# Causal attention weighs the values with unsplit exponentials in full 32-bit products on 32 rows

## The reference, cut to what matters

```python
qkv = hidden_states @ Wqkv            # 4 batches, 512 tokens, 512 features
q = qkv[..., :512].reshape(4, 512, 32, 16)          # 32 heads of 16
k = qkv[..., 512:528]                 # one key head and
v = qkv[..., 528:]                    # one value head for all
scores = jnp.einsum('bqhd,bkd->bhqk', q, k) * 16 ** -0.5
scores = jnp.where(causal, scores + alibi, -1e30)
probs = jax.nn.softmax(scores, axis=-1)
attn = jnp.einsum('bhqk,bkd->bqhd', probs, v).reshape(4, 512, 512)
x = x + attn @ Wo
```

## Time and profile before

| | |
|---|---|
| Median of 3 runs | 3246.93 us (3245.48 to 3249.31) |
| Profiled execution, span | 3252.0 us |
| Causal attention's units, 4 batches | from 118 to 728 us of the span |
| Feed-forward, first | about 760 to 1227 us |
| Window attention | about 1227 to 2785 us |
| TensorE busy in the whole span | 2840.8 us, 87% |
| Granted TensorE clock, mean | 0.936 of full speed |

### The profile page before, as it was taken

One profiled execution on the slowest core, in us unless ns is written; L12 is line 12 of the kernel. 1 busy time (PEld: TensorE's weight loads), 2 busy tenths in 40 slices (PEclk: granted clock), 3 DMA queues, 4 the chain that ended last, 5 costly groups with the idle time before them and its releaser, 6 DMA issues. The chain is left out here.

```text
span 3252.0 us, 44782 instructions
## 1 busy us (share of the span) xinstructions
PE 2840.8 (87%) x14364; PEld 2215.5 (68%) x14404; DVE 2248.5 (69%) x4342; ACT 1390.3 (43%) x2947; POOL 1253.5 (39%) x938
## 2 busy tenths in 40 slices
PE   3798888984988896999999997799999999699888
PEld 2564545543766774788888885688888887577666
DVE  3656565644877775878787774778777787577776
ACT  2477666772322224444444443444444444232222
POOL 2266454561422222444444441444444442242221
PEclk7699988986999998999999998999999999799999
DMA  4231414224000001111010010011111100300001
GB/s 151 62 95 33 130 32 124 40 53 136 1 1 1 0 0 54 33 33 32 26 32 10 29 33 27 7 33 33 32 32 32 32 19 1 96 1 1 0 0 52
DMA packets 148429, 125.24 MB, mean 39 GB/s; under 512 B 18644, under 2 KB 117972, under 8 KB 148276
## 3 DMA queue, kind: packets, MB, share of 16 engines
q1 hardware_dynamic: 148308, 123.75, 13.7%
HBM read 96.71 MB, written 27.26 MB: 38 GB/s over the span
## 5 line engine op out<-in xcount | busy, mean ns | idle before, releaser
L1273 POOL TENSOR_TENSOR a_probs_low<-a_probs,a_probs_high 128x512 fp32r<-128x512 f32 x240 | 309.3, 1297 | 329.0 <-ACT a_probs_high L1193 328.0
L1944 POOL TENSOR_TENSOR rope_straight<-rope_straight,rope_crossed 128x512 f32<-128x512 f32 x160 | 206.9, 1293 | 477.8 <-DVE rope_crossed L1755 477.8
L634 POOL TENSOR_TENSOR f_hidden_low<-f_hidden,f_hidden_high 128x512 fp32r<-128x512 f32 x112 | 144.7, 1292 | 552.5 <-ACT f_hidden_high L579 552.5
L1049 DVE TENSOR_REDUCE a_max<-a_max_scores 128x1 f32<-128x384 f32 (+3 forms) x352 | 215.7, 637 | 153.4 <-PE a_max_scores L924 149.7
L1849 ACT ACTIVATE probs<-probs,exp_bias 128x256 f32<-128x256 f32 (+1 forms) x512 | 240.8, 471 | 168.4 <-DVE exp_bias L1737 168.1
L1596 PE MATMUL proj<-y_high,wq_high 128*128 128x512 f32 x512 | 213.3, 417 | 26.3 <-DVE y_low L1725 17.1
L1191 ACT ACTIVATE a_probs<-a_scores 128x512 f32<-128x512 f32 x320 | 192.7, 602 | 97.7 <-PE a_scores L937 48.4
L1596 PE MATMUL w_sum<-o_high,wo_high 128*128 128x512 f32 x512 | 204.2, 399 | 7.6 <-DVE xt L1779 4.7
L1910 ACT CAST probs_turned_high<-probs_turned 128x896 fp32r<-128x896 f32 x128 | 116.3, 908 | 211.9 <-PE probs_turned L1638 211.9
L1856 ACT CAST q_high<-rope_straight 128x512 fp32r<-128x512 f32 x128 | 79.5, 621 | 292.4 <-POOL rope_straight L1944 292.4
L1596 PE MATMUL proj<-y_low,wq_high 128*128 128x512 f32 x512 | 204.0, 399 | 0.0
(11 more groups left out here) (256 smaller groups left out, 8674.1 us busy)
## 6 DMA issues: line engine op xcount, KB each, us to landing
a_queries<-a_q_stacked SPq DMA_DIRECT2D x16, 1024.0 KB, 7.1
wq_raw<-in_L_attn_b_wq SPq DMA_DIRECT2D x32, 512.0 KB, 3.7
wo_raw<-in_L_attn_b_wo SPq DMA_DIRECT2D x16, 1024.0 KB, 6.2
a_q_stacked<-a_q_part_high SPq DMA_DIRECT2D x32, 256.0 KB
a_out_parts<-a_out SPq DMA_DIRECT2D x128, 64.0 KB
f_w_raw<-in_L_ffn_w SPq DMA_DIRECT2D x28, 256.0 KB, 5.3
f_w_raw<-in_L_ffn_w2t SPq DMA_DIRECT2D x14, 512.0 KB, 7.9
a_z<-a_out_parts SPq DMA_DIRECT2D x12, 512.0 KB
```

The costliest lines, as they stand in the source:

```text
L1049: e.tensor_reduce(to, scores, AX.X, ALU.max).then_inc(s["max_read"], 1)
L1273: e.tensor_tensor(pl[:, g % 4], pf[:, g % 4], f32(ph[:, g % 4]), ALU.subtract)\
L1944: e.tensor_tensor(ra[:, slot], ra[:, slot], rb[:, slot], ALU.add).then_inc(roped, 1)
```

## The change

The exponentials are no longer split. ScalarE makes one exponential for each unit, of type float32, and nothing is subtracted from it. The values are no longer split either: the tile has 32 columns, 0 to 15 the values and 16 to 31 ones. TensorE multiplies the two float32 tiles in one product per unit, where two products of float32r tiles stood. The result has one part and its sum in row 16; one store, one load and one addition less follow from that.

```diff
-VROWS = 80
+VROWS = 32
...
-        o_dram = nc.dram_tensor("a_out_parts", [NB, 2, AH * AD, S], F32).ap()
+        o_dram = nc.dram_tensor("a_out_raw", [NB, AH * AD, S], F32).ap()
...
-        vs, vn = sb("a_values", [P, ST, VROWS], F32R), sb("a_values_next", [P, ST, VROWS], F32R)
+        vs, vn = sb("a_values", [P, ST, VROWS]), sb("a_values_next", [P, ST, VROWS])
...
         pf = sb("a_probs", [P, 4, S])
-        ph, pl = (sb(f"a_probs_{x}", [P, 4, S], F32R) for x in ("high", "low"))
...
-                e.wait_ge(*split_by(b, g))
-                for x in (ph, pl):
-                    mm = e.matmul(obank[hg % 2][0:VROWS, :], vs[:, kt, :], x[:, g % 4, :], start=kt == 0 and x is ph,
-                                  stop=kt == qt and x is pl)
-                mm.then_inc(s["pv_done"], 1)
+                e.wait_ge(s["exp_done"], b.it * UB + g + 1)
+                e.matmul(obank[hg % 2][0:VROWS, :], vs[:, kt, :], pf[:, g % 4, :], start=kt == 0, stop=kt == qt)\
+                    .then_inc(s["pv_done"], 1)
...
-            def low_probs(b, g):
-                e.wait_ge(s["exp_done"], b.it * UB + g + 1)
-                e.tensor_tensor(pl[:, g % 4], pf[:, g % 4], f32(ph[:, g % 4]), ALU.subtract)\
-                    .then_inc(s["low_by_vector"], 1)
...
-                chain(e.tensor_tensor(at[:, 0], at[:, 0], at[:, 1], ALU.add))
-                e.tensor_tensor(at[:, 0], at[:, 0], at[:, 2], ALU.mult).then_inc(s["at_ready"], 1)
+                e.tensor_tensor(at[:, 0], at[:, 0], at[:, 1], ALU.mult).then_inc(s["at_ready"], 1)
...
-                if g >= 4 or not b.first:
-                    before = (b, g - 4) if g >= 4 else (Batch(b.it - 1), g - 4 + UB)
-                    e.wait_ge(*split_by(*before))
-                e.activation(pf[:, g % 4], sbank[g % 2][:, :], ACT.Exp)
                 wait(e, s["pv_done"], b.it * UB + g - 3)
-                e.activation(ph[:, g % 4], sbank[g % 2][:, :], ACT.Exp).then_inc(s["exp_done"], 1)
+                e.activation(pf[:, g % 4], sbank[g % 2][:, :], ACT.Exp).then_inc(s["exp_done"], 1)
...
-                        if g % 4 != 1:
-                            low_probs(b, g)
...
-                for c in range(2):
-                    to = o_dram[bass.ds(b.it, 1), c, tile * P:(tile + 1) * P, qt * P:(qt + 1) * P]\
-                        .rearrange("b (h d) q -> d (b h) q", d=AD)
-                    e.dma_start(to, ot[32 * c:32 * c + AD, tile % 2].rearrange("p a h q -> p (a h) q"))\
-                        .then_inc(o_stored[tile % 2], 16)
+                to = o_dram[bass.ds(b.it, 1), tile * P:(tile + 1) * P, qt * P:(qt + 1) * P]\
+                    .rearrange("b (h d) q -> d (b h) q", d=AD)
+                e.dma_start(to, ot[0:AD, tile % 2].rearrange("p a h q -> p (a h) q")).then_inc(o_stored[tile % 2], 16)
...
-                e.dma_start(at[:, 0:2, :], o_dram[bass.ds(b, 1), :, m * P:(m + 1) * P, :].rearrange("b c p t -> p (b c) t"))\
+                e.dma_start(at[:, 0, :], o_dram[bass.ds(b, 1), m * P:(m + 1) * P, :].rearrange("b p t -> (b p) t"))\
```

More of the change, by code:

```diff
@@ L705, in causal_attention @@
         with ExitStack() as late:
-            last_at = sb_in(nc, late)("a_last_out", [P, DT, 3, S])
+            last_at = sb_in(nc, late)("a_last_out", [P, DT, 2, S])
         qa = sb("a_queries", [P, PAIRS, S], F32R)
@@ L716, in causal_attention @@
         vt = sb("a_v_by_dim", [AD, S])
-        at = zf[:, 0:3]
+        at = zf[:, 0:2]
         sums = sb("a_sums_tile", [P, AH * S // P])
@@ L726, in causal_attention @@
         misc = [ps(f"a_misc{i}", [P, S]) for i in range(2)]
-        names = ("max_full", "max_read", "scores_full", "exp_done", "low_by_vector", "low_by_pool", "pv_done", "o_copied",
-                 "misc_used", "m_high", "m_low", "kv_high", "kv_low", "vt_copied", "v_high", "v_low", "q_high", "q_low",
+        names = ("max_full", "max_read", "scores_full", "exp_done", "pv_done", "o_copied",
+                 "misc_used", "m_high", "m_low", "kv_high", "kv_low", "vt_copied", "v_high", "q_high", "q_low",
                  "k_landed", "keys_kept", "x_summed", "sq_ready", "sq_added", "centred", "seed", "z_ready", "zh_ready", "zl_ready",
@@ L821, in group_end @@
             return qt * HG + hg if kt == qt else None
[L823 to L827, removed]
         def wait(e, sem, value):
@@ L991, in read_small @@
                     e.wait_ge(s["v_high"], b.ahead() + 1)
-                    e.tensor_tensor(vn[:, :, 32:32 + AD], bank[:, 0:ST * AD].rearrange("p (t d) -> p t d", t=ST),
-                                    f32(vn[:, :, 0:AD]), ALU.subtract).then_inc(s["v_low"], 1)
-                    e.wait_ge(s["v_low"], b.ahead() + 1)
                     e.sem_inc(free, 1)
@@ L1080, in keep_keys @@
                 e.tensor_copy(ka[1][:, :], kan[1][:, :]).then_inc(s["keys_kept"], 1)
-                e.wait_ge(s["v_low"], b.it + 1)
+                e.wait_ge(s["v_high"], b.it + 1)
                 e.tensor_copy(vs[:, :, :], vn[:, :, :]).then_inc(s["keys_kept"], 1)
             def body(b):
-                chain = Chain(e, s["dve_step"], 3 if b.first else b.it * 7 - 1)
+                chain = Chain(e, s["dve_step"], b.it * 3 + 3)
                 keep_keys(b)
@@ L1103, in body @@
                             if OUT <= g < OUT + OUT_STEP * DT and (g - OUT) % OUT_STEP == 0:
-                                out_tile((b.it - 1) * DT + (g - OUT) // OUT_STEP, chain)
+                                out_tile((b.it - 1) * DT + (g - OUT) // OUT_STEP)
                             if OUT < g <= OUT + OUT_STEP * DT and (g - OUT) % OUT_STEP == 1:
@@ L1109, in body @@
                         read_small(b, *x, chain)
-                    if kind == "scores" and x[0] % 4 == 2:
-                        low_probs(b, x[0] - 1)
             first = Batch(None)
@@ L1119, in _ @@
                 if x[0] == "Vt":
-                    e.wait_ge(s["cleared"], 4)
+                    e.wait_ge(s["cleared"], 3)
                 for j in range(GROUPS[x[1] % ST]) if x[0] == "mT" else ():
@@ L1136, in _ @@
             batches(e, body)
-            chain = Chain(e, s["dve_step"], 7 * NB - 4)
+            chain = Chain(e, s["dve_step"], 3 * NB)
             invert_sums(NB - 1)
             for m in range(DT):
-                out_tile((NB - 1) * DT + m, chain, last_at[:, m], last_landed[m])
+                out_tile((NB - 1) * DT + m, last_at[:, m], last_landed[m])
             for m in range(DT):
@@ L1199, in copy_out @@
                 if hg % 2 == 0:
-                    wait(e, o_stored[hg // 2 % 2], 48 * (b.it * 2 * ST + group_end(g) // 4))
+                    wait(e, o_stored[hg // 2 % 2], 32 * (b.it * 2 * ST + group_end(g) // 4))
                 e.copy(ot[:, hg // 2 % 2, hg % 2], obank[hg % 2][0:VROWS, :].rearrange("p (h q) -> p h q", h=4))\
@@ L1296, in _ @@
                 sum_squares(first, n)
-            e.memset(f32(vn[:, :, 0:64]), 0.0).then_inc(s["cleared"], 1)
-            e.memset(f32(vn[:, :, 64:VROWS]), 1.0).then_inc(s["cleared"], 1)
+            e.memset(vn[:, :, AD:VROWS], 1.0).then_inc(s["cleared"], 1)
             for d in range(DT):
```

12 lines of the change are left out of this document (4 added, 8 removed).

## The result

The changed kernel takes 3322.85 us (median of 4 runs, 3322.25 to 3323.48); the kernel before took 3248.12 us beside it (3245.48 to 3252.44). The ratio is 1.0226, with an interval of 1.0212 to 1.0239: 74.7 us slower, where 34 us were forecast. The profiled execution has a span of 3320.4 us.

A forecast was written before the change was run, and what follows sets the result against it. TensorE was taken as busiest but also waiting in causal attention. Terms +112 - 53 - 7 - 5 - 6 gave +41 us, a second account +27; the middle, +34, gave 3281 us, range 3257 to 3317 (chance 0.69), outer range 3243 to 3345.

The forecast's parts named there:

- The product: TensorE's weighing in causal attention: one float32 product costs 0.35 us a unit more than the pair, +112 us over 320 units.
- The change of shape: Switching TensorE between 32-column and 128-column stationary tiles: taken as 0, with 20 us kept for the range.
- The first rival, the drain: Every product drains TensorE, 0.25 to 0.35 us each, 80 to 112 us in all; 3361 to 3393 us; chance 0.10.
- The waits and slack: TensorE's waits for other engines in the attention stage give back 53 us, slack in short pieces 7 us.
- The sign I gave: In the changed profile, TensorE's listed waits in the stage should fall from 82 to about 35 us.
- The clock: Half speed on some 105 us of the stage costs about 35 us; 5 us taken back, bounds 0 and 35.
- three causes for half speed: Half speed comes at batch starts and behind long waits; three of its causes were said to stay.
- The tail: After the last batch: half the a_out bytes, no addition and no last units' subtraction save 6 us.
- The short slack: Where ScalarE pressed as hard as TensorE, some 65 units gain 0.1 us each, 7 us.
- The second rival: Faster: exchange between engines sets the stage, all waits and half speed go; -29 us, 3218 us; chance 0.08.
- three signs of being wrong: L943's two records under 0.7 us; next instruction over 0.1 us late as a rule; half speed far from 105 us.

The follow-up runs named there:

- e4: Kernel before (two float32r products, 80 columns) with one exponential, no subtractions, low parts left out: 3155.9 us, ratio 0.9697.
- e6: Changed kernel with the values' stationary tile padded from 32 to 80 columns, still one float32 product a unit: 3243.4 us, ratio 0.9962 to the kernel before.
- e3: Changed kernel with exponentials and values in float32r, each unit weighed twice with the same 32-column tiles: 3158.7 us, ratio 0.9700 to the kernel before.
- e5: Changed kernel, 32 columns, with two units' weighings back to back after every odd unit: 3295.0 us, ratio 1.0118 to the kernel before.

## Why the prediction went as it did

The direction held, the likeliest size did not: 34 us forecast, 75 measured, inside the range. Point by point:

- **The product, +112 us.** Right: 108 to 115 us by e4 and e6, 0.453 us from record to record for 0.43.
- **The change of shape, 0.** This step failed. The prediction took L903's hand-over in 0.03 us as what a 32-column tile costs, and gave "the new product has 512 in each of several passes" as the reason why even less would show. L903 is a transpose. The reading of its row was right: it runs without a gap in the changed kernel too, at all 14 places. (In the kernel before only 2 of 14 show the 0.03 us; at 10 others L937 starts just 0.05 us after an exponential has ended, so it waits for ScalarE there, though no gap is listed.) But the row is of another kind of instruction. The product of float32 on 32 columns pays 0.09 us ahead (0.160 for 0.066 in e6) and 0.20 us behind (0.523 + 0.34 us for 0.028 + 0.64), 0.30 us in all. Unit by unit, where both traces are at full clock and without a wait, the changed kernel takes 0.30 us more than e6 too (300 units). The stage got 79 us longer for it, not 96, in part because TensorE idles 8.5 us less. The row nearest to it was L898: a float32 product with a stationary tile of 16 rows by 128 columns, so narrow the other way, with the same shape of price: it starts 0.10 us late, and the product behind it takes 0.38 us for 0.23.
- **The first rival, the drain,** had the mechanism, at 0.25 to 0.35 us a product and 80 to 112 us. Its time, 3361 to 3393 us, is too long mainly because the relief was undersized: the drain itself measured 79. I gave it 0.10 since "the neighbour with 32 columns and 128 rows shows none of it". I had weighed the shape and never the type or the kind of the product.
- **The waits and slack, -60 us.** About right. TensorE idles 66 us less in e6 than before (16.0 us, against 609.8 - 527.3 = 82.5 us of the stage; some 40 missing records of before may make up to 10 us of that). The relief by itself, in e4, brought 43; the rest went because the longer product covers waits. The sign I gave, 82 to 35 us of listed waits, came out as 82 to 9 in after, and 19 in e6.
- **The clock, -5 us.** This step failed as well. Half speed fell from 108 us of the stage to 4, and did not stay at "about 105". If TensorE streams all the while, 104 us less are worth 52 us; at the two thirds that the prediction used, 35. What the balance of e6's stage leaves for it agrees: +108 to +115 for the product and -66 for idle time give -3.9 only with -46 to -53 for the clock (10 us more if before's missing records are counted as work). The prediction kept three causes for half speed, but the row to ask was that of the stretch with TensorE full: clock 1.00. e4, with the relief and without the added work, keeps 36 us of half speed, so 72 of the 104 us went with the relief; with float32 (e6) it is 5, so the added work took 31 more.
- **The tail, -6 us.** 5.5 us.
- **The short slack, -7 us.** The prediction counted "some 65 units" for 24 of the first batch and the last batch; a batch alone has 80, so it is 104. At its own 0.1 us each that is 10 us for 7, too little to matter.
- **The second rival,** with a chance of 0.08, had the relief nearly right: all waits and all half speed come back. e6, which is the change without the drain, is 12 us faster than before, where that rival said 29.

Two of the three signs of being wrong that the prediction named came up: the instruction behind the product is over 0.1 us late as a rule (0.976 us after the first record, for 0.86), and half speed left its 105 us.

In sum, without the drain the forecast of +34 would have met -12 us (e6), 46 us lower, mostly by the clock. This hid more than half of the missed drain, and that the time fell inside the range is owed to it, which is luck: 34 - 46 + 79 = 67, and the rest up to 75 is that these kernels were timed in different groups (by the ratios, e6 and after are 2.64% or 86 us apart).

The Trainium skill, "TensorEngine Tiling (Array Packing)", Key Properties, says that changing the tiling mode drains the engine, and its Tiling Modes list 128 by 32 and 128 by 64, but none between 64 and 128 columns. The traces agree with it for float32: gaps on 32 and 64 columns, none on 80 and 128. They have none for float32r on 32 columns (e3). The Trainium skill, "PSUM — Partial Sum Buffer", The four PSUM rules, remarks that float32r matmuls force the mask of column groups to the full one; if so, e3 never left the full mode, and L951 never did. No run shows the mask, but with the two remarks together the weighing comes out on each of its four widths and in both types as they would have it. They leave open why the transposes L903 and L896, float32 on 32 columns, show no gap next to L937 and L930. That the lost time is a drain of the engine is the Trainium skill's word for it; the traces show only when instructions start. The prediction had the first rule and set it aside by one row of another kind of instruction.

## What to carry to other kernels

Don't let a float32 product stand on a stationary tile of 64 columns or fewer between products of the full width. Pad it with columns that nobody reads (80 cost nothing here and gave 79 us), or put such products side by side, since the change is paid and not the product (two products in a row paid once; the price of longer rows wasn't measured). Before a row stands in for a new instruction, compare the type and the kind of the operation as well as the shape; and where a change makes TensorE continuously busy, count the half speed that goes away, at up to half of its time.

## What the runs showed of the hardware

- A plain float32 product of 128 rows by 512 moving columns has two records, 0.45 us apart, and holds TensorE some 0.85 us at full clock (0.34 more than the pair's 0.51), against 0.23 us for one of float32r. The number of stationary columns changes little in that (0.453, 0.480, 0.445 and 0.485 us between the records for 32, 64, 80 and 128).
- A float32 product on 32 or 64 columns between float32r and bf16 products of the full width loses about 0.09 us ahead and 0.20 us behind, and the next load isn't started early. The records span this time and count it as busy. A float32 transpose on 32 columns loses nothing next to a full-width float32r product (0.03 to 0.04 us, e4 and after), nor do float32r products on 32 columns (e3).
- Two units' products of that kind behind each other pay once (0.251 us in e5 for each time, 0.256 us in after).
- The stage with TensorE continuously at work has 4 us at half speed in 685, the same stage with waits has 108 in 610.
- A wait can leave no gap in the list: in the kernel before, L937 starts 0.17 to 0.27 us after L903 where it waits for an exponential, and 0.03 us where it doesn't, and in both cases L903's record reaches up to it.
